# The guard of the q and k norms moves from a GpSimd clamp into VectorE's normalising instruction, as a minimum with 1e12

## The chip, the cores and the metric

The kernel runs on one core of a Trainium2 chip. The metric is the device time of one execution in microseconds (us), as a median of runs. The engines are TensorE (PE; PEld is its loading of weights), VectorE (DVE), ScalarE (ACT), GpSimd (POOL) and SyncE (SP, which only starts DMAs here). Each engine runs its own instructions in program order and waits for others at semaphores.

## The reference, cut to what matters

A residual block over 2048 tokens of width 128: softmax attention, a stack of local attention and feed-forward layers, linear attention, and the same stack again. One stack has six layers, and each layer first does this:

```
qkv = shift_tokens(x) @ Wqkv                    # 16 heads of 64
q = q / max(norm(q), 1e-12) * q_scale           # norm over the 64 elements of a head
k = k / max(norm(k), 1e-12) * k_scale
q, k = rotary(q, k)
attn = softmax(8 * q @ k^T over a window of 32 keys before and up to the token)
x = (attn @ v) @ Wo + x
```

A feed-forward layer follows. The change concerns the two lines with `max(norm, 1e-12)`, in both stacks (named f and g in the profile): twelve layers in all.

## The kernel before

`local_stack` does one stack. Its attention part goes over 16 tiles of 128 tokens, and over four steps (c = 0 to 3) in each tile: a step handles 8 heads of q or k (512 columns), in the order q, k, q, k. So a layer has 64 steps, numbered n = 4t + c, and the twelve layers have 768. The work is a software pipeline written out by hand: in step n every engine does a piece for step n, and later pieces for steps before it, always in the same order. All tiles on the way have two buffers (`b = c % 2`).

The chain of one step, by tile names:

- PE multiplies x by a slice of `wqkv` into `ps_qk` (L1171).
- ACT squares it into `sq` (L991), DVE sums the squares of each head into `ss`, 128x8 (L1083).
- POOL clamps: `sg = max(ss, 1e-24)` (L928), and takes `rn = sg ^ -0.5` (L931). An increment of `pl_sg` and a wait for it stand between the two.
- DVE normalises: `qh = ps_qk * rn`, with `rn` repeated over the 64 elements of a head (L1070). Then it makes the two rotary products `t1` and `t2` (L1097, L1099).
- POOL adds them into `qr` (L936). PE transposes `qr` (L1240), and ACT copies that into `qT` or `kT` (L1016, L1018, L1020).
- PE writes the mask and the scores (L1187, L1194), DVE takes the maximum `nmx` (L1076), ACT the exponentials `ex` (L1005), DVE the reciprocal `rd` and the product `pn` (L1087, L1090), PE transposes `pn` (L1176), ACT copies it to `pT` (L987), PE multiplies by v (L1232), ACT copies the result to `aT` (L1027).

In one step the orders of the engines are:

- DVE: `qh` of n-1, `nmx` of n-4, `ss` of n, `rd` and `pn` of n-5, `t1` and `t2` of n-1. Once a tile (c = 0) `xr` stands ahead of `qh` (L1066).
- POOL: `sg` of n, `rn` of n, `qr` of n-1.
- PE: `wqkv` product of n, transposes of `pn` of n-6, mask and scores of n-4, then in c = 0 and 2 a product for v (L1207), in c = 1 a transpose of x (L1160), in c = 3 the product with `wo` (L1214, 16 instructions), then the product with v of n-7 (L1232) and the transposes of `qr` of n-2 (L1240).
- ACT: copy of `pT`, squares, in c = 0 and 2 the copy of v, exponentials, copy of `qT` or `kT`, copy of `aT`.

The first 11 steps of a layer have no `wo` product, and the first few none of the later pieces. The mask and the scores in c = 0 and c = 2 wait for a copy to `kT`.

Of the kernel before, what the change touches and what calls it, by code (L numbers as in the profile page):

```python
# [9 lines left out]
ALU = mybir.AluOpType  # L10
# [3 lines left out]
P = 128  # L14
# [5 lines left out]
DH = 64  # L20
# [604 lines left out]
def local_stack(nc, tag, w, consts, xf, xa):  # L625
# [6 lines left out]
    with ExitStack() as ctx:  # L632
        sems, per_layer, ahead = [], {}, {}

        def sb(name, shape, dt=F32):
            return ctx.enter_context(nc.sbuf_tensor(f"{tag}_{name}", shape, dt))

        def sem(name, each=0, start=0):

            s = ctx.enter_context(nc.semaphore(f"{tag}_{name}"))  # L640
            sems.append(s)
            per_layer[s.num], ahead[s.num] = each, start
            return s

        def upto(s, L, n, by=1):

            return L * per_layer[s.num] + (n * by + (by + ahead[s.num]))

        def bank(i, n=1):
# [5 lines left out]
        ps_qk = banks[0:2]  # L655
# [29 lines left out]
        xT = sb("xT", [P, 2, P])  # L685
        sq = sb("sq", [P, 2, 512])
        ss = sb("ss", [P, 2, 8])
        sg = sb("sg", [P, 2, 8])
        rn = sb("rn", [P, 2, 8])
        qh = sb("qh", [P, 2, 512])  # L690
        t1 = sb("t1", [P, 2, 512])
# [39 lines left out]
        pe_v, act_v = sem("pe_v", 2 * NT, 3), sem("act_v", 2 * NT, 1)  # L731

        pe_qkv, act_sq, dv_ssq = sem("pe_qkv", STEPS), sem("act_sq", STEPS), sem("dv_ssq", STEPS, 2)
        pl_sg, pl_rn, dv_qh, dv_t2, pl_qr = (sem("pl_sg", STEPS), sem("pl_rn", STEPS, 2), sem("dv_qh", STEPS, 2),
                                             sem("dv_t2", STEPS), sem("pl_qr", STEPS, 2))
        pe_qkT, act_kprev, act_qk = sem("pe_qkT", STEPS, 2), sem("act_kprev", STEPS // 2), sem("act_qk", STEPS, 1)

# [165 lines left out]
        @block.gpsimd  # L903
        def _(pool):
            for s in (pl_rn, pl_qr):
                pool.sem_inc(s, ahead[s.num])
            pool.memset(minus_half[:], -0.5).then_inc(zeroed, 1)
            pool.memset(kT[:], 0.0).then_inc(zeroed, 1)

            def fold_rope(n, kind):  # L910

                pool.wait_ge(ld_scales, upto(ld_scales, n, 0, 32))
                whole = qk_scales[:, kind, :].unsqueeze(1).broadcast_to([P, NT, DH])
                halves = qk_scales[:, kind, :].rearrange("p (a b) -> p a b", a=2)[:, ::-1, :]
                pool.tensor_tensor(rope[:, 2 * kind, :, :], rope0[:, 2 * kind, :, :], whole, ALU.mult).then_inc(pl_rope, 1)
                for a in range(2):
                    sl = slice(a * 32, a * 32 + 32)
                    pool.tensor_tensor(rope[:, 2 * kind + 1, :, sl], rope0[:, 2 * kind + 1, :, sl],
                                       halves[:, a, :].unsqueeze(1).broadcast_to([P, NT, 32]),
                                       ALU.mult).then_inc(pl_rope, 1)  # L920

            def tile(L, t, q):
                for c in range(4):
                    n, b = 4 * t + c, c % 2
                    if real(t, c, 0):

                        pool.wait_ge(dv_ssq, upto(dv_ssq, L, n)).then_inc(own["pool"], 1)
                        pool.tensor_scalar(sg[:, b, :], ss[:, b, :], 1e-24, None, ALU.max).then_inc(pl_sg, 1)  # L928
                        pool.wait_ge(pl_sg, upto(pl_sg, L, n))
                        pool.wait_ge(dv_qh, upto(dv_qh, L, n - 2))  # L930
                        pool.tensor_tensor(rn[:, b, :], sg[:, b, :], minus_half[:], ALU.pow).then_inc(pl_rn, 1)  # L931
                    if real(t, c, 1):

                        pool.wait_ge(dv_t2, upto(dv_t2, L, n - 1))
                        pool.wait_ge(pe_qkT, upto(pe_qkT, L, n - 3))
                        pool.tensor_tensor(qr[:, 1 - b, :], t1[:, 1 - b, :], t2[:, 1 - b, :], ALU.add).then_inc(pl_qr, 1)  # L936

            def inverse_std(L, m, q):
                pool.wait_ge(dv_mv, upto(dv_mv, L, m)).then_inc(own["pool"], 1)
                pool.tensor_scalar(var[:, q, :], mv[:, q, :, 1], 1e-5, None, ALU.add).then_inc(pl_var, 1)  # L940
                pool.wait_ge(pl_var, upto(pl_var, L, m))
                pool.tensor_tensor(rstd[:, q, :], var[:, q, :], minus_half[:, 0:FT], ALU.pow).then_inc(pl_rstd, 1)

            def group(L, m, q):
                known = isinstance(m, int)
                if known and m == 0:
                    inverse_std(L, 0, 0)
                if not known or m + 1 < NF:
                    inverse_std(L, m + 1, 1 - q)
                if not known or 0 <= m - 2 < NF:  # L950

                    pool.wait_ge(ld_wf, upto(ld_wf, L, 0, 13 * 16))
                    pool.wait_ge(ld_f[q], upto(ld_f[q], L, (m - 2) >> 1, 16))
                    pool.tensor_tensor(fx[:, q, :, :], fx[:, q, :, :], b2[:].unsqueeze(1).broadcast_to([P, FT, D]),
                                       ALU.add).then_inc(pl_b2, 1)
                if known and m < 2:
                    pool.wait_ge(dv_t2, upto(dv_t2, L, STEPS - 1))
                    fold_rope(L + 1, m)

            pool.wait_ge(zeroed, 5)  # L960
            pool.wait_ge(ld_rope, 16)
            fold_rope(0, 0)
            fold_rope(0, 1)
            with pool.Fori(0, DEPTH) as L:
                layer(pool, tile, group, L, NT + 1)
# [88 lines left out]
        def _(dve):  # L1054
# [5 lines left out]
            def tile(L, t, q):  # L1060
                for c in range(4):
                    n, b = 4 * t + c, c % 2
                    if c == 0 and real(t - 3, 0, 0):
                        dve.wait_ge(pe_Wo, upto(pe_Wo, L, t - 3))
                        dve.wait_ge(ld_r[1 - q], upto(ld_r[1 - q], L, (t - 3) >> 1, 16))
                        dve.tensor_tensor(xr[:, 1 - q, :], ps_y[:, 0:P], xr[:, 1 - q, :], ALU.add).then_inc(dv_y, 1)  # L1066
                    if real(t, c, 1):

                        dve.wait_ge(pl_rn, upto(pl_rn, L, n - 1))
                        dve.tensor_tensor(heads(qh[:, 1 - b, :]), heads(ps_qk[1 - b][:]),  # L1070
                                          rn[:, 1 - b, :].unsqueeze(2).broadcast_to([P, 8, DH]), ALU.mult).then_inc(dv_qh, 1)
                    if real(t, c, 4):

                        dve.wait_ge(pe_s, upto(pe_s, L, n - 4))
                        dve.wait_ge(act_exp, upto(act_exp, L, n - 6))
                        dve.tensor_reduce(nmx[:, b, :].rearrange("p (h j) -> p h j", h=2),  # L1076
                                          ps_s[:, :, 0:2 * KEYS].rearrange("p h (j c) -> p h j c", j=2), AX.X, ALU.max,
                                          negate=True).then_inc(dv_max, 1)
                    if real(t, c, 0):

                        dve.wait_ge(act_sq, upto(act_sq, L, n))
                        dve.wait_ge(pl_rn, upto(pl_rn, L, n - 2))
                        dve.tensor_reduce(ss[:, b, :], heads(sq[:, b, :]), AX.X, ALU.add).then_inc(dv_ssq, 1)  # L1083
                    if real(t, c, 5):

                        dve.wait_ge(act_exp, upto(act_exp, L, n - 5))
                        dve.reciprocal(rd[:, 1 - b, :], sm[:, 1 - b, :]).then_inc(dv_rd, 1)  # L1087
                        dve.wait_ge(dv_rd, upto(dv_rd, L, n - 5))
                        dve.wait_ge(pe_pT, upto(pe_pT, L, n - 7))
                        dve.tensor_tensor(pn[:, 1 - b, :, :], ex[:, 1 - b, :, :],  # L1090
                                          rd[:, 1 - b, :].unsqueeze(2).broadcast_to([P, 4, KEYS]), ALU.mult).then_inc(dv_pn, 1)
                    if real(t, c, 1):

                        tj, cj = t + (c - 1) // 4, (c - 1) % 4
                        dve.wait_ge(dv_qh, upto(dv_qh, L, n - 1))
                        dve.wait_ge(pl_qr, upto(pl_qr, L, n - 3))
                        dve.tensor_tensor(heads(t1[:, 1 - b, :]), heads(qh[:, 1 - b, :]),  # L1097
                                          rope[:, 2 * KIND[cj], row(tj), :].broadcast_to([P, 8, DH]), ALU.mult)
                        dve.tensor_tensor(split(t2[:, 1 - b, :]), split(qh[:, 1 - b, :])[:, :, ::-1, :],  # L1099
                                          rope[:, 2 * KIND[cj] + 1, row(tj), :].broadcast_to([P, 8, DH]).rearrange(  # L1100
                                              "p h (a b) -> p h a b", a=2), ALU.mult).then_inc(dv_t2, 1)
# [599 lines left out]
```

## Time and profile before

| what | value |
|---|---|
| median of 3 runs | 5555.81 us (5553.79 to 5558.2) |
| the profiled execution | 5558.9 us |
| its span, first to last instruction | 5557.1 us |
| PE busy | 4778.2 us, 86% |
| DVE busy | 3995.7 us, 72% |
| ACT busy | 3633.8 us, 65% |
| POOL busy | 3288.9 us, 59% |

The span is what the rows below are read from. "Busy" counts an engine's own instructions. The costliest single line of the page is L931 on POOL: 744.8 us in each stack. The two stacks run from about 985 to 3160 us and from about 3365 to 5540 us.

### The profile page before, as it was taken

The page shows a single profiled execution, that of the slowest core. Times are in us where ns is not written, and L with a number is a line of the kernel's source. Part 1 is how long each engine was busy: PE and PEld are TensorE (multiplying, and loading weights), DVE is VectorE, ACT ScalarE, POOL GpSimd, SP SyncE. Part 2 cuts the span into 40 slices and gives each one's busy share as a digit, 9 for nine tenths or more (in the row PEclk, how much of TensorE's full clock was granted, in tenths as well). Part 3 has the DMA queues.
Part 4 walks back from the last instruction along what each step waited for, and adds up shares of the span by engine and source line. Part 5 has one row for each costly group of instructions (what it writes and reads, how often), then busy time and mean ns, then how long its engine had stood idle before and what let it go on. Part 6 is the DMA issues. An engine that isn't in the chain of part 4 may idle for free. (4 is left out here: it accounts for less than half of the span.)

```text
span 5557.1 us, 149601 instructions
## 1 busy us (share of the span) xinstructions
PE 4778.2 (86%) x45702; PEld 2962.8 (53%) x45796; DVE 3995.7 (72%) x8097; ACT 3633.8 (65%) x11776; POOL 3288.9 (59%) x2876
## 2 busy tenths in 40 slices
PE   5999998797998988979889666989989889798896
PEld 1333332465665665656656454655656656566565
DVE  7888885676776767767767546767767777677675
ACT  1777776675775757757667405757757667577674
POOL 3000000785876858858678406858858678587684
PEclk6999999899999999999999878999999999999998
DMA  0000000222222222222222202222222222222223
GB/s 13 1 2 1 2 1 16 80 56 73 50 65 65 50 74 55 50 74 56 69 56 57 79 6 83 57 74 50 66 65 51 74 57 53 71 56 66 61 53 89
DMA packets 332331, 288.41 MB, mean 52 GB/s; under 512 B 149102, under 2 KB 290964, under 8 KB 329748
## 3 DMA queue, kind: packets, MB, share of 16 engines
q1 hardware_dynamic: 331028, 281.93, 19.7%
q8 instruction: 254, 4.16, 0.3%
q14 instruction: 281, 2.30, 0.1%
q10 hardware_dynamic: 768, 0.02, 0.0%
HBM read 100.42 MB, written 30.41 MB: 24 GB/s over the span
## 5 line engine op out<-in xcount | busy, mean ns | idle before, releaser
L931 POOL TENSOR_TENSOR g_rn<-g_sg,g_minus_half 128x8 f32<-128x8 f32 x384 | 744.8, 1940 | 32.0
L931 POOL TENSOR_TENSOR f_rn<-f_sg,f_minus_half 128x8 f32<-128x8 f32 x384 | 744.8, 1939 | 32.0
L425 DVE TENSOR_REDUCE a_maxima<-a_max 128x1 f32<-128x512 f32 x1024 | 651.5, 686 | 148.4 <-PE a_max L539 111.3
L1005 ACT ACTIVATE g_ex<-g_bank,g_nmx 128x96 f32<-128x96 f32 x1536 | 502.6, 342 | 235.1 <-DVE g_nmx L1076 235.1
L1005 ACT ACTIVATE f_ex<-f_bank,f_nmx 128x96 f32<-128x96 f32 x1536 | 502.6, 342 | 234.6 <-DVE f_nmx L1076 234.5
L349 ACT ACTIVATE a_pex<-a_scores 128x512 f32<-128x512 f32 x1024 | 531.9, 607 | 160.2 <-PE a_scores L548 159.2
L1070 DVE TENSOR_TENSOR f_qh<-f_bank,f_rn 128x512 f32<-128x512 f32 x384 | 265.6, 692 | 370.5 <-POOL f_rn L931 370.5
L1070 DVE TENSOR_TENSOR g_qh<-g_bank,g_rn 128x512 f32<-128x512 f32 x384 | 265.6, 692 | 370.5 <-POOL g_rn L931 370.5
L936 POOL TENSOR_TENSOR f_qr<-f_t 128x512 f32<-128x512 f32 x384 | 485.6, 1265 | 11.5 <-DVE f_t L1099 11.5
L936 POOL TENSOR_TENSOR g_qr<-g_t 128x512 f32<-128x512 f32 x384 | 485.6, 1264 | 11.5 <-DVE g_t L1099 11.5
L1171 PE MATMUL g_bank<-g_wqkv,g_xT 128*128 128x512 f32 x768 | 410.5, 617 | 33.0 <-ACT g_xT L979 24.6
L1171 PE MATMUL f_bank<-f_wqkv,f_xT 128*128 128x512 f32 x768 | 410.2, 617 | 31.9 <-ACT f_xT L979 24.3
L928 POOL TENSOR_SCALAR f_sg<-f_ss 128x8 f32<-128x8 f32 x384 | 219.8, 572 | 339.0 <-DVE f_ss L1083 339.0
L928 POOL TENSOR_SCALAR g_sg<-g_ss 128x8 f32<-128x8 f32 x384 | 219.8, 572 | 337.4 <-DVE g_ss L1083 337.4
L280 POOL COPY a_v_head<-a_v_all 128x128 f32 (+1 forms) x16 | 4.6, 293 | 695.1 <-PE a_sums L557 695.1
L1240 PE MATMUL g_bank<-g_ident,g_qr 128*128 128x128 f32 x1536 | 254.1, 288 | 133.3 <-POOL g_qr L936 133.3
L1240 PE MATMUL f_bank<-f_ident,f_qr 128*128 128x128 f32 x1536 | 253.4, 288 | 132.9 <-POOL f_qr L936 132.9
L539 PE MATMUL a_max<-a_stackT 128*128 128x512 bf16 x963 | 347.6, 397 | 20.8 <-DVE a_maxima L425 12.6
L548 PE MATMUL a_scores<-a_stackT 128*128 128x512 bf16 x991 | 308.8, 382 | 27.7 <-ACT a_pex L349 20.6
L1005 ACT ACTIVATION_READ_ACCUMULATOR g_ex<-g_bank,g_nmx 128x1 f32 x1536 | 318.2, 207 | 0.0
L1005 ACT ACTIVATION_READ_ACCUMULATOR f_ex<-f_bank,f_nmx 128x1 f32 x1536 | 318.1, 207 | 0.0
L1083 DVE TENSOR_REDUCE f_ss<-f_sq 128x8 f32<-128x512 f32 x384 | 259.5, 676 | 49.0 <-ACT f_sq L991 35.0
(240 smaller groups left out, 12390.7 us busy)
## 6 DMA issues: line engine op xcount, KB each, us to landing
f_vw<-f_vt SPq DMA_DIRECT2D x96, 384.0 KB, 4.3
g_vw<-g_vt SPq DMA_DIRECT2D x96, 384.0 KB, 4.3
f_vw<-f_vt SPq DMA_DIRECT2D x96, 256.0 KB, 3.6
g_vw<-g_vt SPq DMA_DIRECT2D x96, 256.0 KB, 3.6
f_vw<-f_vt SPq DMA_DIRECT2D x96, 128.0 KB, 2.3
g_vw<-g_vt SPq DMA_DIRECT2D x96, 128.0 KB, 2.3
f_wqkv<-in_f_Wqkv_dram SPq DMA_DIRECT2D x7, 1536.0 KB, 9.3
g_wqkv<-in_f_Wqkv_dram SPq DMA_DIRECT2D x7, 1536.0 KB, 9.5
```

The source lines that it names most:

```text
L349: act.activation(pex[:, kt % 2, i % NG, :], ps_s[i % 3][:], ACT.Exp).then_inc(act_ex, 1)
L425: dve.tensor_reduce(maxima[:, m // 4, m % 4:m % 4 + 1], ps_max[m % 3][:], AX.X, ALU.max).then_inc(dv_max, 1)
L539: pe.matmul(ps_max[m % 3][:], stackT[:, slot, 0, P * (m // 4):P * (m // 4) + P], stackT[:, slot, 1, GQ * (m % 4):GQ * (m % 4) + GQ], start ...
L548: pe.matmul(ps_s[i % 3][:], stackT[:, slot, 1, P * kt:P * kt + P], stackT[:, slot, 0, GQ * g:GQ * g + GQ], start=True, stop=True).then_inc ...
L928: pool.tensor_scalar(sg[:, b, :], ss[:, b, :], 1e-24, None, ALU.max).then_inc(pl_sg, 1)
L931: pool.tensor_tensor(rn[:, b, :], sg[:, b, :], minus_half[:], ALU.pow).then_inc(pl_rn, 1)
L936: pool.tensor_tensor(qr[:, 1 - b, :], t1[:, 1 - b, :], t2[:, 1 - b, :], ALU.add).then_inc(pl_qr, 1)
L1005: last = act.activation(ex[:, b, u, :], ps_s[:, h, KEYS * jj:KEYS * jj + KEYS], ACT.Exp, bias=nmx[:, b, u:u + 1], accum_out=sm[:, b, u:u + 1])
L1070: dve.tensor_tensor(heads(qh[:, 1 - b, :]), heads(ps_qk[1 - b][:]), rn[:, 1 - b, :].unsqueeze(2).broadcast_to([P, 8, DH]), ALU.mult).then_ ...
L1083: dve.tensor_reduce(ss[:, b, :], heads(sq[:, b, :]), AX.X, ALU.add).then_inc(dv_ssq, 1)
L1171: pe.matmul(ps_qk[b][:], xT[:, q, :], wqkv[:, at:at + 512], start=True, stop=True).then_inc(pe_qkv, 1)
L1240: last = pe.transpose(ps_qkT[:, P * j:P * j + P], qr[:, b, P * j:P * j + P], ident[:])
```

## The change

POOL's clamp, its tile `sg` and its semaphore are gone; POOL raises `ss` itself to -0.5. DVE's normalising instruction takes the minimum of `rn` and 1e12 before it multiplies. It was a TENSOR_TENSOR with the PSUM tile as its first input and `rn` as its second; it is now a SCALAR_TENSOR_TENSOR with `rn` as its first input, the constant 1e12, and the PSUM tile as its second.

```diff
-        sg = sb("sg", [P, 2, 8])
...
-        pl_sg, pl_rn, dv_qh, dv_t2, pl_qr = (sem("pl_sg", STEPS), sem("pl_rn", STEPS, 2), sem("dv_qh", STEPS, 2),
+        pl_rn, dv_qh, dv_t2, pl_qr = (sem("pl_rn", STEPS, 2), sem("dv_qh", STEPS, 2),
...
                         pool.wait_ge(dv_ssq, upto(dv_ssq, L, n)).then_inc(own["pool"], 1)
-                        pool.tensor_scalar(sg[:, b, :], ss[:, b, :], 1e-24, None, ALU.max).then_inc(pl_sg, 1)
-                        pool.wait_ge(pl_sg, upto(pl_sg, L, n))
                         pool.wait_ge(dv_qh, upto(dv_qh, L, n - 2))
-                        pool.tensor_tensor(rn[:, b, :], sg[:, b, :], minus_half[:], ALU.pow).then_inc(pl_rn, 1)
+                        pool.tensor_tensor(rn[:, b, :], ss[:, b, :], minus_half[:], ALU.pow).then_inc(pl_rn, 1)
...
-                        dve.tensor_tensor(heads(qh[:, 1 - b, :]), heads(ps_qk[1 - b][:]),
-                                          rn[:, 1 - b, :].unsqueeze(2).broadcast_to([P, 8, DH]), ALU.mult).then_inc(dv_qh, 1)
+                        dve.scalar_tensor_tensor(out=heads(qh[:, 1 - b, :]), in0=rn[:, 1 - b, :].unsqueeze(2).broadcast_to([P, 8, DH]),
+                                                 scalar=1e12, in1=heads(ps_qk[1 - b][:]), op0=ALU.min, op1=ALU.mult).then_inc(dv_qh, 1)
```

## Rows read from the trace of the kernel before

**Rows 1.** Chain of waits over the span: waiter, releaser, us in total, times, longest.

```profile
DVE f_qh L1070 <- POOL f_rn L931: 370.5, 384, 2.2
```

**Rows 2.** Timeline of DVE, steady steps: start, duration, engine, line, names, shapes, idle before.

```profile
1203.21 0.69 DVE L1070 TENSOR_TENSOR f_qh<-f_bank,f_rn 128x512 f32<-128x512 f32 x1 [0.95 <-POOL f_rn L931]
...
1204.29 0.68 DVE L1083 TENSOR_REDUCE f_ss<-f_sq 128x8 f32<-128x512 f32 x1
...
1205.08 0.56 DVE L1090 TENSOR_TENSOR f_pn<-f_ex,f_rd 128x384 f32<-128x384 f32 x1
1205.56 0.68 DVE L1097 TENSOR_TENSOR f_t<-f_qh,f_rope 128x512 f32<-128x512 f32 x1
...
1207.80 0.69 DVE L1070 TENSOR_TENSOR f_qh<-f_bank,f_rn 128x512 f32<-128x512 f32 x1 [0.95 <-POOL f_rn L931]
...
1216.97 0.69 DVE L1070 TENSOR_TENSOR f_qh<-f_bank,f_rn 128x512 f32<-128x512 f32 x1 [0.95 <-POOL f_rn L931]
```

**Rows 3.** Timeline of POOL in the same step.

```profile
1205.16 0.58 POOL L928 TENSOR_SCALAR f_sg<-f_ss 128x8 f32<-128x8 f32 x1 [0.75 <-DVE f_ss L1083]
1205.83 1.94 POOL L931 TENSOR_TENSOR f_rn<-f_sg,f_minus_half 128x8 f32<-128x8 f32 x1
1207.74 1.27 POOL L936 TENSOR_TENSOR f_qr<-f_t 128x512 f32<-128x512 f32 x1
```

**Rows 4.** Timeline of POOL and DVE, first two steps of a layer.

```profile
996.46 0.25 POOL L928 TENSOR_SCALAR f_sg<-f_ss 128x8 f32<-128x8 f32 x1 [1.18 <-DVE f_ss L1083]
996.79 1.67 POOL L931 TENSOR_TENSOR f_rn<-f_sg,f_minus_half 128x8 f32<-128x8 f32 x1
...
999.97 0.50 POOL L928 TENSOR_SCALAR f_sg<-f_ss 128x8 f32<-128x8 f32 x1 [1.52 <-DVE f_ss L1083]
...
1000.29 0.68 DVE L1099 TENSOR_TENSOR f_t<-f_qh,f_rope 128x512 f32<-128x512 f32 x1
...
1000.56 1.94 POOL L931 TENSOR_TENSOR f_rn<-f_sg,f_minus_half 128x8 f32<-128x8 f32 x1
```

**Rows 5.** Timeline of PE over one tile of steady steps.

```profile
1204.50 0.66 PE L1240 MATMUL f_bank<-f_ident,f_qr 128*128 128x128 f32 x4
...
1209.02 0.69 PE L1232 MATMUL f_bank<-f_pT,f_vw 128*64 128x64 f32 x16
1209.64 0.66 PE L1240 MATMUL f_bank<-f_ident,f_qr 128*128 128x128 f32 x4
...
1213.85 0.66 PE L1240 MATMUL f_bank<-f_ident,f_qr 128*128 128x128 f32 x4
...
1216.64 0.69 PE L1232 MATMUL f_bank<-f_pT,f_vw 128*64 128x64 f32 x16
1218.31 0.65 PE L1240 MATMUL f_bank<-f_ident,f_qr 128*128 128x128 f32 x4 [0.98 <-POOL f_qr L936]
...
1220.42 0.34 PE L1187 MATMUL f_bank<-f_mask_bf,f_ident_bf 128*128 128x192 bf16 x2 [0.16 <-ACT f_kT L1020]
...
1222.85 0.66 PE L1240 MATMUL f_bank<-f_ident,f_qr 128*128 128x128 f32 x4
```

**Rows 6.** Windows of the steady part: us, busy by engine, PE clock, DMA.

```profile
1150.00:1278.00 128.00, 119.79 (x1376) 80.09 (x1376) 101.84 (x202) 99.68 (x369) 105.36 (x84) 1.00 0.22 54
```

**Rows 7.** Timeline of ACT in the step after the `wo` product.

```profile
1212.22 0.60 ACT L991 ACTIVATE f_sq<-f_bank 128x512 f32<-128x512 f32 x1
```

**Rows 8.** Groups of DVE by line and shape: count, busy us, mean ns, idle before.

```profile
L1140 DVE SCALAR_TENSOR_TENSOR g_ag<-g_bank,g_b,g_gl 128x256 f32<-128x256 f32 x96 | 45.9, 483 | 80.6 <-ACT g_gl L1041 80.6
...
L1130 DVE TENSOR_TENSOR g_fy<-g_bank,g_fx 128x256 f32<-128x256 f32 x48 | 20.2, 422 | 16.4 <-DMA xf<-g_fy 11.5 <-PE g_bank L1271 3.1 <-POOL g_fx L954 1.8
...
L1483 DVE TENSOR_SCALAR b_kp<-b_bank 128x512 f32<-128x512 f32 x16 | 11.1, 692 | 13.0 <-PE b_bank L1590 13.0
```

**Rows 9.** Timeline of DVE and of POOL in a feed-forward part.

```profile
1309.96 1.26 DVE L1140 SCALAR_TENSOR_TENSOR f_ag<-f_bank,f_b,f_gl 128x256 f32<-128x256 f32 x3 [3.17 <-ACT f_gl L1041]
...
1310.40 2.48 POOL L918 TENSOR_TENSOR f_rope<-f_rope,f_qk_scales 128x512 f32<-128x512 f32 x2
```

## The prediction

> **What bounds the kernel now.** I read the waits first, then the timelines of DVE and POOL over a few steps, then PE's. The waits say where the changed lines stand: DVE waits for `rn` before every `qh`, 370.5 us in 384 steps of a stack [rows 1], 741 us in both. Whether that idle time is the bound, the timeline must say. It does: one `qh` starts at 1203.21, the next at 1207.80, a period of 4.59 us [rows 2], and the same period holds in practically every steady step, whatever PE has to do in it. Follow what ends last: `ss` starts 1.08 after `qh`; POOL's `sg` starts 0.87 after `ss`, at 1205.16, and ends at 1205.74; the power runs from 1205.83 to 1207.77; `qh` follows at 1207.80 [rows 2, 3]. So the step is a closed loop of DVE and POOL, with the clamp in it: 1.08 + 0.87 + 0.58 + 0.09 + 1.94 + 0.03 = 4.59. DVE idles 0.95 in it; its own work is 3.64 a step.
>
> PE is nearly as full: 119.79 of 128 us, at a granted clock of 1.00, that is 2.4 GHz [rows 6]. Its starts give what it needs when nothing holds it. A tile is four steps: 5.14 us with the `wo` product (1204.50 to 1209.64), 4.21 with a v product (to 1213.85), 3.40 with the transpose of x (to 1216.64 + 0.62, the 0.62 as from 1209.02 to 1209.64), and 4.21 again (the trace shows 4.54, 1218.31 to 1222.85, with a wait of 0.33 for `kT` inside) [rows 5]. Sum 16.96 against 18.36 for four periods. PE has only 1.40 us of idle time in a tile, and the loop can't gain more there.
>
> **What goes, and what it costs: POOL.** How long the power takes depends on DVE. In a layer's first step DVE is idle and the clamp takes 0.25, the power 1.67. In the second step the clamp takes 0.50 and the power 1.94; that power starts at 1000.56, under a product with two SBUF inputs that ends at 1000.97, and ends 1.53 after that [rows 4]. In the steady step the clamp starts 0.08 after `pn` and ends 0.10 after `pn` ends (1205.64); the power starts under `t1`, which ends at 1206.24, and again ends 1.53 later, though `t2` follows `t1` without a gap [rows 2, 3]. So a POOL instruction that meets a DVE instruction with two SBUF inputs is held until that one ends, and slips in before the next one.
>
> Without the clamp the power takes its place, at 1205.16, and is held by `pn` in place of `t1`. It ends at 1205.64 + 1.53 = 1207.17, and `qh` starts at 1207.20: 0.60 earlier, period 3.99, and 2.91 from `ss` to `qh`. The bounds for the gain of the loop: if it took 1.94 from its start, 0.67; if 1.67, 0.94; if it had to wait for `t1` after all, nothing (a rival below). I take 0.60, since three pairs of rows fit it. The semaphore and the wait that go too lie inside the 0.09. `qr` comes as early after `qh` as before, since POOL starts it when the power ends; POOL's load falls from 3.8 to 3.3 a step. No DMA or wait is added.
>
> The Trainium skill, "SBUF — State Buffer", section "Who interferes with whom", says that a DVE instruction with two SBUF inputs contends with a GpSimd instruction that reads SBUF, and that one with at most one SBUF input doesn't. The trace agrees with the first half by 0.25 against 0.50. By the page's other half the new `qh`, with one input in PSUM, stays clear of `qr`.
>
> **What is added: DVE.** `qh` takes 0.692 as a TENSOR_TENSOR; the trace has no 512-wide SCALAR_TENSOR_TENSOR. A 256-wide one with a pointer scalar takes 483 ns against 422 for a TENSOR_TENSOR of that size, 61 more; a two-operation TENSOR_SCALAR with constants, from PSUM, takes 692 at 512 [rows 8]. So the new one costs 0.69 if the 61 ns belong to the pointer and 0.75 if they don't. I take 0.69, the row with constants; 0.75 makes the loop 4.05. Below 0.69 I see no reason, as the elements are as many.
>
> **What is late next.** If only the loop counted, a layer would gain 0.33 in its first step (clamp plus gap) and 0.60 in 63 more, 38.1 us, or 458 us in twelve layers: 5101. PE doesn't allow it. Its tile of 16.96 is longer than 4 x 3.99 = 15.96. And it can't be quite dense, for one chain goes round through all engines once a tile. From the mask of c = 2 PE needs 2.43 to the end of its step (1220.42 to 1222.85) and 5.14 for the step with `wo`. From there the squares of c = 0 end 3.18 later (1209.64 to 1212.82) [rows 5, 7]; 0.03 on, `ss` starts, then 2.91 to `qh`. And 3.45 after `qh`, by way of `nmx`, exponentials and `kT`, comes the next mask of c = 2 (1216.97 to 1220.42) [rows 2, 5]. Sum: 2.43 + 5.14 + 3.21 + 2.91 + 3.45 = 17.14. Before, it was 17.74 and hidden under 18.36. A steady tile gains 18.36 - 17.14 = 1.22, not 2.40.
>
> **Sum.** A layer has 64 steps. First step 0.33. Steps 2 to 11 have no `wo` product; a tile of PE without it is about 15 us, under 15.96, so each gains the loop's 0.60: 6.0. The other 53 steps are 13.25 tiles, at 1.22: 16.2. At the end of the attention part PE is about 0.8 further behind DVE than before (the chain above puts it there; an estimate), and that is paid in the drain. 0.33 + 6.0 + 16.2 - 0.8 = 21.7 a layer, 260 us in twelve. Feed-forward parts, both other attentions and DMAs only shift. The profiled execution took 5558.9 with a span of 5557.1, 3.1 above the median shown: 5558.9 - 260 = 5299, or 5296 by the median. I predict 5296.
>
> Bounds: with PE dense (16.96) and nothing paid in the drain, 0.33 + 6.0 + 18.6 = 24.9 a layer, 5257. With `qh` at 0.75, the early steps gain 0.54 and the chain is 17.20: 20.3 a layer, 5312. The likeliest case alone: 5250 to 5345.
>
> **Rivals.**
>
> *No slack between PE and the loop.* Then each step costs the longer of the two: 5.14 + 4.21 + 3.99 + 4.21 = 17.55. Gain 0.33 + 6.0 + 13.25 x 0.81 - 0.8 = 16.3 a layer: 5361. For it speaks that the engines share two buffers only; against it, that the loop today holds 4.59 through a PE step of 5.14.
>
> *The new instruction runs at half rate.* 256 elements more cost 270 ns in rows 8 (692 - 422), so 512 at half rate add 0.54. The loop becomes 4.53, a gain of 0.06 a step, about 46 us: 5510. The skill's "Vector Engine (DVE) Microarchitecture Reference", section "Points that are easy to get wrong", says that this form halves its throughput with two SBUF sources that aren't bf16. Here one source is in PSUM, so by its letter the rule doesn't apply, and no row shows the case.
>
> *The change doesn't do what it says.* If the power must wait for `t1` although it starts under `pn`, it ends where it ends now, and nothing moves: 5556. Against it: the clamp, and the power in rows 2 and 3, slip in between two such products.
>
> *Slower: the new `qh` collides with `qr`.* POOL starts `qr` 0.06 before `qh`, for 1.27. If the new form, with `rn` as its first input, is held until `qr` ends, each step grows by 1.21: 3.99 + 1.21 = 5.20, 0.61 longer than now, 468 us in 768 steps: 6024. It decides from 0.60 us more in `qh`. Against it: three instructions of this form, one input in PSUM and one in SBUF, take 1.26 in all while POOL works on `rope` [rows 9]. Only the places of the inputs are swapped.
>
> **Chances.** Forecast 0.70; no slack 0.13; half rate 0.07; nothing moves 0.04; collision 0.04; the rest, 0.02, for something slower unseen. The range runs from 5245, just under PE dense, to 5400, beyond the case without slack, and leaves out the last four: 0.17. Within 0.2% (11 us) is what can't be told from no change. Faster 0.90, same 0.04, slower 0.06.
>
> **What the profile after must show.** POOL's power about 2.0 long, ending 1.53 after `pn`; `qh` at 0.69; 2.91 from `ss` to `qh` when nothing else holds it. The period no longer constant: four steps of about 17.1, a gap of a few tenths before the mask of c = 2, `ss` waiting for `sq` or `nmx` for the scores after the `wo` step. DVE's wait for `rn` down from 0.95 to about 0.35 a step, and PE's busy share up. Wrong it would be if `qh` were longer, if `ss` waited in most steps, or if the clock fell below 1.00 in the denser stretch.

## The result, and the profile after

The kernel after takes 5336.36 us as a median of 4 runs (5324.37 to 5340.76), the kernel before 5557.01 (5553.79 to 5559.11). The ratio is 0.960, with a 95% interval of 0.9583 to 0.9617. 5296 was forecast, 40 us lower; the gain is 221 us where 260 was forecast.

The page of the kernel after, its parts 1 and 5 (busy us, share of the span, instructions; then line, engine, names, count, busy us, mean ns, idle before):

```profile
span 5333.0 us, 148063 instructions
...
PE 4757.5 (89%) x45702; PEld 2949.2 (55%) x45796; DVE 4038.5 (76%) x8097; ACT 3633.9 (68%) x11776; POOL 2862.2 (54%) x2108
...
L928 POOL TENSOR_TENSOR f_rn<-f_ss,f_minus_half 128x8 f32<-128x8 f32 x384 | 750.8, 1955 | 459.7 <-DVE f_ss L1080 371.0
...
L1067 DVE SCALAR_TENSOR_TENSOR f_qh<-f_rn,f_bank 128x512 f32<-128x512 f32 x384 | 264.0, 687 | 133.3 <-POOL f_rn L928 122.6
...
L1073 DVE TENSOR_REDUCE f_nmx<-f_bank 128x4 f32<-128x384 f32 x384 | 213.0, 555 | 127.5 <-PE f_bank L1191 126.1
```

POOL lost 768 instructions, the clamps, and 427 us of busy time. The others do the same work in a shorter span. The new instruction takes 687 ns, the old one 692. DVE's wait for `rn` fell from 370.5 us a stack [rows 1] to 122.6, and DVE now waits 126.1 us for the scores, as the prediction said it would after the `wo` step. A window inside the steady part of both kernels, before and after (columns as in rows 6; the window of rows 6 itself reaches beyond the steady part of the kernel after, whose last `qh` of that layer starts at 1264.2):

```profile
1100.00:1228.00 128.00, 120.03 (x1378) 80.07 (x1376) 101.84 (x203) 99.82 (x370) 105.02 (x84) 1.00 0.22 54
...
1100.00:1228.00 128.00, 126.66 (x1459) 84.92 (x1457) 110.07 (x217) 105.86 (x393) 94.65 (x61) 1.00 0.24 58
```

PE works 126.66 of 128 us where it was 120.03; the granted clock is 1.00 in both, the level of 2.4 GHz.

The loop of DVE and POOL, in steps where PE holds nothing up (timeline of the kernel after; start, duration):

```profile
1202.33 0.56 DVE L1087 TENSOR_TENSOR f_pn<-f_ex,f_rd 128x384 f32<-128x384 f32 x1
...
1202.50 1.90 POOL L928 TENSOR_TENSOR f_rn<-f_ss,f_minus_half 128x8 f32<-128x8 f32 x1 [1.08 <-PE f_bank L1237]
...
1204.43 0.69 DVE L1067 SCALAR_TENSOR_TENSOR f_qh<-f_rn,f_bank 128x512 f32<-128x512 f32 x1 [0.33 <-POOL f_rn L928]
...
1205.50 0.68 DVE L1080 TENSOR_REDUCE f_ss<-f_sq 128x8 f32<-128x512 f32 x1
...
1206.29 0.56 DVE L1087 TENSOR_TENSOR f_pn<-f_ex,f_rd 128x384 f32<-128x384 f32 x1
1206.36 2.00 POOL L928 TENSOR_TENSOR f_rn<-f_ss,f_minus_half 128x8 f32<-128x8 f32 x1 [0.72 <-DVE f_ss L1080]
...
1208.39 0.69 DVE L1067 SCALAR_TENSOR_TENSOR f_qh<-f_rn,f_bank 128x512 f32<-128x512 f32 x1 [0.33 <-POOL f_rn L928]
```

From `ss` to `qh` it is 1208.39 - 1205.50 = 2.89 (2.91 foreseen), and the period 1208.39 - 1204.43 = 3.96 (3.99). The power starts 0.17 after `pn` in one step and 0.07 after it in the next, and takes 1.90 and 2.00: its end is 1.51 after the end of `pn` both times. So it is held by `pn`, as worked out. (The releaser "PE f_bank L1237" in the second row is an inference by time; by the code that instruction waits for DVE alone. Where the profile names an engine that the code doesn't, the code decides.)

I read the starts of `qh` of the first layer of the first stack, before and after, into this table ("tile" is the 60th start less the 12th, over 12):

| | before | after | foreseen after |
|---|---|---|---|
| first `ss` to first `qh` | 2.91 | 2.59 | 2.58 |
| next 11 steps | 48.7 | 41.95 | about 42.4 (ten at 0.60 less, one at 1.22 / 4) |
| a steady tile of four steps | 18.35 | 17.35 | 17.14 |
| periods in a tile | four of 4.59 | 3.96, 3.96, 5.20, 4.21 | not all alike |
| last `qh` to the next layer's first `ss` | 70.9 | 72.1 | 0.8 more |

The layer went from 361.1 to 342.1 us. One row of the table is off: the tile, by 0.2 us.

### The profile page after: what moved, and what is told of

It is laid out like the page before. It is cut to its first block and busy times, and to the rows that moved or that the text cites. A ratio compares the mean times of both kernels' runs of the same rounds, so it can differ in the third digit from the quotient of the medians.

```text
span 5333.0 us, 148063 instructions
## 1 busy us (share of the span) xinstructions
PE 4757.5 (89%) x45702; PEld 2949.2 (55%) x45796; DVE 4038.5 (76%) x8097; ACT 3633.9 (68%) x11776; POOL 2862.2 (54%) x2108
## 5 line engine op out<-in xcount | busy, mean ns | idle before, releaser
L928 POOL TENSOR_TENSOR g_rn<-g_ss,g_minus_half 128x8 f32<-128x8 f32 x384 | 750.9, 1956 | 464.0 <-DVE g_ss L1080 379.5
L928 POOL TENSOR_TENSOR f_rn<-f_ss,f_minus_half 128x8 f32<-128x8 f32 x384 | 750.8, 1955 | 459.7 <-DVE f_ss L1080 371.0
L1002 ACT ACTIVATE f_ex<-f_bank,f_nmx 128x96 f32<-128x96 f32 x1536 | 505.6, 349 | 42.4 <-DVE f_nmx L1073 41.3
L933 POOL TENSOR_TENSOR g_qr<-g_t 128x512 f32<-128x512 f32 x384 | 486.1, 1266 | 17.7 <-DVE g_t L1096 17.7
L933 POOL TENSOR_TENSOR f_qr<-f_t 128x512 f32<-128x512 f32 x384 | 486.1, 1266 | 17.7 <-DVE f_t L1096 17.7
L1067 DVE SCALAR_TENSOR_TENSOR g_qh<-g_rn,g_bank 128x512 f32<-128x512 f32 x384 | 264.0, 688 | 133.3 <-POOL g_rn L928 122.6
L1067 DVE SCALAR_TENSOR_TENSOR f_qh<-f_rn,f_bank 128x512 f32<-128x512 f32 x384 | 264.0, 687 | 133.3 <-POOL f_rn L928 122.6
L1073 DVE TENSOR_REDUCE g_nmx<-g_bank 128x4 f32<-128x384 f32 x384 | 213.0, 555 | 132.8 <-PE g_bank L1191 131.3
L1073 DVE TENSOR_REDUCE f_nmx<-f_bank 128x4 f32<-128x384 f32 x384 | 213.0, 555 | 127.5 <-PE f_bank L1191 126.1
L1080 DVE TENSOR_REDUCE g_ss<-g_sq 128x8 f32<-128x512 f32 x384 | 260.5, 678 | 51.5 <-ACT g_sq L988 34.3
L1229 PEld LDWEIGHTS g_bank<-g_pT,g_vw 128*64 128x64 f32 x6144 | 210.3, 137 | 157.5 <-issue 129.6
```

Of the source, the lines that this page charges most:

```text
L928: pool.tensor_tensor(rn[:, b, :], ss[:, b, :], minus_half[:], ALU.pow).then_inc(pl_rn, 1)
L1002: last = act.activation(ex[:, b, u, :], ps_s[:, h, KEYS * jj:KEYS * jj + KEYS], ACT.Exp, bias=nmx[:, b, u:u + 1], accum_out=sm[:, b, u:u + 1])
L1067: dve.scalar_tensor_tensor(out=heads(qh[:, 1 - b, :]), in0=rn[:, 1 - b, :].unsqueeze(2).broadcast_to([P, 8, DH]), scalar=1e12, in1=heads(p ...
L1229: last = pe.matmul(ps_o[r, at:at + BLK], vw[:, p, blk, P * j + DH * h:P * j + DH * h + DH], pT[:, 1 - b, 2 * h + jj, BLK * blk:BLK * blk + ...
```

## The experiments

Each ratio below is to runs of the kernel before that were taken with it. "Tile" is measured as above, in the first layer of each kernel's own profile; it is the same within 0.02 in all twelve layers.

**Which chain holds the tile.** The timeline after, over one tile. These rows make up one chain (L976, in c = 1, is ACT's copy of the transposed x into `xT`):

```profile
1194.03 0.66 PE L1237 MATMUL f_bank<-f_ident,f_qr 128*128 128x128 f32 x4
...
1196.56 1.12 PE L1204 MATMUL f_bank<-f_wqkv,f_xT 128*128 128x512 f32 x2
...
1197.89 0.59 ACT L996 COPY f_vt<-f_bank 128x512 f32<-128x512 f32 x1 [0.69 <-PE f_bank L1204]
...
1200.28 0.56 PE L1191 MATMUL f_bank<-f_kT,f_qT 64*64 64x96 f32 x16
...
1200.91 0.56 DVE L1073 TENSOR_REDUCE f_nmx<-f_bank 128x4 f32<-128x384 f32 x1
...
1201.35 0.29 ACT L976 COPY f_xT<-f_bank 128x128 f32<-128x128 f32 x1
1201.51 0.38 ACT L1002 ACTIVATE f_ex<-f_bank,f_nmx 128x96 f32<-128x96 f32 x1
...
1202.79 0.33 ACT L1015 COPY f_kT<-f_kT 128x128 f32<-128x128 f32 x1
...
1203.15 0.59 ACT L1017 COPY f_kT<-f_bank 128x512 f32<-128x512 f32 x1
...
1203.79 0.34 PE L1184 MATMUL f_bank<-f_mask_bf,f_ident_bf 128*128 128x192 bf16 x2 [0.19 <-ACT f_kT L1017]
...
1206.22 0.66 PE L1237 MATMUL f_bank<-f_ident,f_qr 128*128 128x128 f32 x4
...
1211.36 0.66 PE L1237 MATMUL f_bank<-f_ident,f_qr 128*128 128x128 f32 x4
```

The prediction had the next mask of c = 2 at 3.45 after a `qh`, since `nmx` follows `qh` at 0.61. Here `qh` starts at 1200.21, but `nmx` only at 1200.91, when the scores of c = 1 end (1200.28 + 0.56). The mask stands 1203.79 - 1194.03 = 9.76 after the end of the `wo` step, not 9.57 (3.21 + 2.91 + 3.45). With 2.43 and 5.14 the chain is 17.33. It doesn't pass through the power at all. Over all twelve layers the `nmx` that follows such a `qh` starts 0.7 after it and 0.07 after the end of the scores; in the kernel before, every `nmx` of the steady steps started 0.61 after its `qh`, and 0.7 us or more after the scores. This is theory A; theory B is the prediction's chain, with something small added.

*POOL adds where it raised to a power (norms left out; q and k are scaled wrongly).*

```diff
-pool.tensor_tensor(rn[:, b, :], ss[:, b, :], minus_half[:], ALU.pow).then_inc(pl_rn, 1)
+pool.tensor_tensor(rn[:, b, :], ss[:, b, :], minus_half[:], ALU.add).then_inc(pl_rn, 1)
```

> GpSimd adds in place of raising to a power, so q and k are scaled wrongly (the norm is left out); GpSimd's instruction falls from about 2.0 us to some 0.6. Theory A, a steady tile is set by a chain that goes from PE's scores of c = 1 over the maximum, the exponentials and the copies to kT to the mask of c = 2 and does not pass through the power: the steady tile stays at 17.3 us, only the first steps of a layer gain, about 4 us a layer: 5336 - 45 = 5290. Theory B, the chain of the prediction, through the squares, the power and qh: the tile falls to PE's 16.96, 0.38 x 13 x 12 = 59 us more: 5231.

Measured: 5307.21 us, ratio 0.9551 (0.9535 to 0.9567). The tile is 17.33. The instruction takes 0.56 where it took 2.00. So a POOL instruction that is far shorter moves the steady tile by nothing, and theory B falls. In the first layer the first `qh` comes 1.42 earlier after the first `ss` and the 11 steps behind it gain 2.05, together 3.5 where about 4 were expected. Over twelve layers the two profiles give 39 us there; 7.5 of them are lost again between the layers, and 29 show in the medians.

*The small copy inside `kT` goes to where ACT waits for v.* It reads and writes only columns whose scores are done by then.

```diff
                         act.activation(sq[:, b, :], ps_qk[b][:], ACT.Square).then_inc(act_sq, 1)
+                    if c % 2 == 0 and real(t, c, 1):
+                        tj, cj = t + (c - 1) // 4, (c - 1) % 4
+                        pairs = slice(4 * HALF[cj], 4 * HALF[cj] + 4)
+                        act.wait_ge(pe_s, upto(pe_s, L, 4 * tj - 3 + 2 * HALF[cj]))
+                        act.copy(kT[:, pairs, 0:WINDOW], kT[:, pairs, P:P + WINDOW]).then_inc(act_kprev, 1)
...
-                            act.copy(kT[:, pairs, 0:WINDOW], kT[:, pairs, P:P + WINDOW]).then_inc(act_kprev, 1)
```

> ACT's small copy inside kT moves from between the exponentials and the kT copy to right after the squares of the step before, where ACT waits for the v product. Theory A: the chain of 17.33 us loses 0.33 and PE's own 16.96 is left: 0.35 x 13 x 12 = 55 us, 5281, and PE's wait before the mask of c = 2 goes from 0.44 to about 0.1. Rival: that wait is filled by another one right behind it (aT, pT or the scores), and the tile stays at 17.3: 5336. Theory B says 17.14 at least as the bound of the power's chain, less 0.33 for the same copy: 5281 too, so this run tells only whether the wait for kT is the bound.

Measured: 5270.54 us, ratio 0.9481 (0.9466 to 0.9497), tile 17.00. This is the fastest version of the study with the whole computation in it, 66 us under the kernel after. By the two profiles 53 of the 66 lie in the steady tiles, where 55 were expected; 8 more lie between the stacks, where the edit changes nothing (see the granted clock there, below). The timeline at the same place:

```profile
1184.79 0.37 ACT L1008 ACTIVATE f_ex<-f_bank,f_nmx 128x96 f32<-128x96 f32 x1
...
1185.11 0.61 ACT L1022 COPY f_kT<-f_bank 128x512 f32<-128x512 f32 x1
...
1185.32 0.60 PE L1178 MATMUL f_bank<-f_ident,f_pn 128*96 128x128 f32 x4
...
1185.78 0.34 PE L1189 MATMUL f_bank<-f_mask_bf,f_ident_bf 128*128 128x192 bf16 x2
```

The copy to `kT` follows the last exponential directly, and the mask follows the transposes of `pn` after 0.46, with no wait named.

*The same edit in the kernel before.*

> The early copy inside kT in the kernel before, with its clamp. The loop of DVE and POOL holds 4.59 a step, the chain through kT is 17.3 a tile and hidden under 18.36: period 4.59, no change, 5557 within 11. If the kT wait had a price of its own in the kernel before, the 66 us that the same edit gave after the change would show here in part.

Measured: 5552.61 us, ratio 0.9993 (0.9984 to 1.0003), period 4.59 throughout. What shortened the tile by 0.35 after the change gives nothing without it: the period is still that of DVE and POOL, and the chain of 17.33 is hidden under 18.36.

**PE's part and ACT's part of it.** Two kernels leave out 15 of the 16 instructions of the product with v (so the attention output is mostly stale in those steps), once in c = 1 and once in c = 0:

```diff
-                        for jj in range(2):
+                        short = c == 1        # c == 0 in the other kernel
+                        for jj in range(1 if short else 2):
...
-                            for blk in range(2):
-                                for h in range(2):
+                            for blk in range(1 if short else 2):
+                                for h in range(1 if short else 2):
```

> PE leaves out 15 of the 16 instructions of the product with v in the steps c = 1, about 0.58 us of its work a tile. In theory A that work stands outside the chain (it comes after the scores of c = 1 and ends before the mask of c = 2 is allowed): tile 17.3, time 5336. Rival C, the tile is PE's work plus a fixed wait, wherever the work stands: 0.58 x 13 x 12 = 90 us less, 5246.

> The same 15 instructions left out in the steps c = 0, where they stand on theory A's chain: that chain falls to 16.75, and the next one, through squares and power (17.12 by the rows of after), takes over: 0.22 x 13 x 12 = 34 us less, 5302. If the power's chain were no bound at all, 0.58 a tile: 5246. Rival C says 5246 here as for c = 1.

Measured: 5329.78 us for c = 1 (ratio 0.9593, 0.9577 to 0.9609; tile 17.35) and 5327.49 for c = 0 (0.9583, 0.9567 to 0.9599; tile 17.32). Neither differs from the kernel after by more than its own runs differ (5324.37 to 5340.76). That the tile is PE's work plus a fixed wait is refuted. But theory A had said 5302 for c = 0, and missed. The timeline of that kernel shows why:

```profile
1181.11 0.58 ACT L996 COPY f_vt<-f_bank 128x512 f32<-128x512 f32 x1 [0.71 <-PE f_bank L1204]
...
1182.43 0.60 PE L1173 MATMUL f_bank<-f_ident,f_pn 128*96 128x128 f32 x4
...
1182.55 0.35 ACT L1002 ACTIVATE f_ex<-f_bank,f_nmx 128x96 f32<-128x96 f32 x1
...
1183.14 0.33 PE L1184 MATMUL f_bank<-f_mask_bf,f_ident_bf 128*128 128x192 bf16 x2
...
1184.56 0.29 ACT L976 COPY f_xT<-f_bank 128x128 f32<-128x128 f32 x1
1184.70 0.39 ACT L1002 ACTIVATE f_ex<-f_bank,f_nmx 128x96 f32<-128x96 f32 x1
```

From the copy of v in c = 0 to the first exponential of c = 1 ACT works without a gap, 3.59 us here and 1201.51 - 1197.89 = 3.62 in the kernel after. PE gained 0.58 and lost most of it at once, since the mask of c = 1 waits for the exponentials of c = 0 (1183.14 is 0.71 after the transposes, not 0.44; counted from the copy of v the mask comes only 0.11 earlier). So two chains are tied there: ACT's own work, and PE's with `nmx`. That is theory A2, and two more kernels test it. In one ACT copies 8 of 128 columns of `pT` in c = 1 (most attention weights stale there); in the other PE's product is short in c = 0 as well.

```diff
-act.copy(pT[0:KEYS, b, :, :], ps_pT[0:KEYS, :].rearrange("p (u q) -> p u q", u=4)).then_inc(act_pT, 1)
+w = 8 if c == 1 else P
+act.copy(pT[0:KEYS, b, :, 0:w], ps_pT[0:KEYS, :].rearrange("p (u q) -> p u q", u=4)[:, :, 0:w]).then_inc(act_pT, 1)
```

> ACT copies 8 of 128 columns of each head's pT in the steps c = 1, so a quarter of the attention weights is left stale; some 0.3 us of ACT's work goes. Theory A2, after the run that shortened PE's product in c = 0 to no effect: from the v product of c = 0 to the mask of c = 2 two chains are tied within 0.05, ACT's own unbroken work (v copy, exponentials, qT, aT, pT, squares, xT, exponentials) and PE's with nmx of c = 1. Shortening ACT's alone moves the tile by 0.05 at most: 17.30 to 17.35, 5336. If ACT's work alone were the bound: 17.05, 0.3 x 13 x 12 = 47 us less, 5289.

> Both at once: 15 of 16 instructions of the product with v left out in c = 0 and pT short in c = 1. Theory A2: both of the tied chains are shorter now; the mask of c = 1 can move only 0.11 earlier, until it waits for the exponentials of c = 0, so the tile falls by about 0.1, to 17.2 (16 us, 5320), more than the sum of the two alone. If something third holds the tile: 17.31 as in the single ones.

Measured: 5329.43 us for ACT alone (0.9592, 0.9576 to 0.9608; tile 17.32), and 5315.88 for both (0.9564, 0.9548 to 0.958; tile 17.20). Each alone moves the tile by 0.03; both together by 0.15, where 0.1 was expected. A2 stands. What holds the tile at 17.20 is in the timeline of that kernel, from a `qh` of c = 1 to the `ss` of c = 0 in the next tile:

```profile
1185.47 0.69 DVE L1068 SCALAR_TENSOR_TENSOR f_qh<-f_rn,f_bank 128x512 f32<-128x512 f32 x1 [0.33 <-POOL f_rn L928]
...
1186.09 0.56 DVE L1074 TENSOR_REDUCE f_nmx<-f_bank 128x4 f32<-128x384 f32 x1
...
1188.93 0.34 PE L1185 MATMUL f_bank<-f_mask_bf,f_ident_bf 128*128 128x192 bf16 x2 [0.16 <-ACT f_kT L1018]
...
1191.37 0.66 PE L1239 MATMUL f_bank<-f_ident,f_qr 128*128 128x128 f32 x4
...
1196.50 0.66 PE L1239 MATMUL f_bank<-f_ident,f_qr 128*128 128x128 f32 x4
...
1199.08 0.60 ACT L989 ACTIVATE f_sq<-f_bank 128x512 f32<-128x512 f32 x1
...
1199.79 0.68 DVE L1081 TENSOR_REDUCE f_ss<-f_sq 128x8 f32<-128x512 f32 x1
```

The mask is back at 3.46 after `qh`, and `nmx` at 0.62. So here the prediction's own chain closes: 2.44 (1188.93 to 1191.37) + 5.13 (to 1196.50) + 3.29 (to 1199.79) + 2.88 (to the next `qh`, 1185.47 + 17.20) + 3.46 = 17.20. Its 3.29 was foreseen as 3.21: `ss` starts 0.11 after the squares end and not 0.03, because DVE is busy with `nmx`, which waited for the scores. PE's chain through the scores arrives at the same time (`nmx` starts 0.07 after them), and no run separates the two.

*The early copy and the short product in c = 1 together.*

> The early copy on top of the change, and the product with v cut to one instruction in c = 1, where it gave nothing without the early copy. If the early copy has made PE's own work the bound (16.96 to 17.0 a tile), the cut counts now: the tile falls until the chain through the power, 17.12 - 0.33 = 16.8, holds it: 0.2 x 13 x 12 = 31 us, 5240. If ACT's work or the kT wait is still the bound at 17.0: 5270.

Measured: 5273.28 us, ratio 0.9488 (0.9473 to 0.9504), tile 16.99, no better than the early copy alone. The mask of c = 2 stands 0.52 after the transposes of `pn` here, where it was 0.46:

```profile
1186.21 0.64 PE L1178 MATMUL f_bank<-f_ident,f_pn 128*96 128x128 f32 x4
...
1186.73 0.34 PE L1189 MATMUL f_bank<-f_mask_bf,f_ident_bf 128*128 128x192 bf16 x2
```

PE saved 0.58 before the transposes of `pn`, but they start 2.90 after the mask of c = 1 (2.97 with the early copy alone), since `qr` and `pn` come no earlier; and the mask stands 0.66 after the copy to `kT` begins (1186.07), as in the kernel after (0.64). So in the fastest version two bounds nearly meet: the chain of A2 less 0.33, at 17.00, and PE's own work, 16.96. What I had expected of the early copy, that it would leave only PE's own work as the bound, was wrong.

**What the parts of the change cost.** Without any guard and with the old DVE instruction, and with both guards (the clamp kept, the new instruction used):

```diff
 # no guard: the kernel after, with the instruction of the kernel before
-dve.scalar_tensor_tensor(..., scalar=1e12, in1=heads(ps_qk[1 - b][:]), op0=ALU.min, op1=ALU.mult)
+dve.tensor_tensor(heads(qh[:, 1 - b, :]), heads(ps_qk[1 - b][:]), rn..., ALU.mult)
 # both guards: the kernel before, with the same two lines the other way round
```

> The change without its minimum: no guard at all, and VectorE keeps the old TENSOR_TENSOR. If the new form costs nothing: as after, 5336, within 11 us. If the form itself gives or takes some hundredths of a us in the loop, that shows in the first 11 steps of a layer alone: at 0.03 a step about 4 us, not to be told.

> The kernel before with VectorE's new instruction, the clamp on GpSimd kept. If all of the gain is GpSimd's: a period of 4.59 and 5557. The first steps gained 0.63 where the sum said 0.60; if the 0.03 are the new instruction's, the period is 4.56 and the time 5557 - 0.03 x 768 = 5534.

Measured: no guard 5325.37 us (5324.13 to 5342.93), ratio 0.9585 (0.9571 to 0.9598), tile 17.35; the interval overlaps that of the kernel after, 0.9583 to 0.9617, and the tile is the same. Both guards 5559.81, ratio 1.0009 (1.0 to 1.0018), periods as in the kernel before, 4.04 in the first three steps of a layer and 4.59 later. So the new instruction costs nothing and gives nothing, and all of the gain is the clamp's. The two medians without and with the minimum differ by 11 us, but the steps don't: 41.95 for the first 11 and 17.35 for a tile in both. The 0.03 by which the loop came out shorter than foreseen isn't the new instruction's. Most of it is the power's: undisturbed it takes 1.65 in both kernels without the clamp, and 1.67 with it. Why is open.

## Why the prediction was right, and what was mis-sized

- *The loop of DVE and POOL is the bound at 4.59, the clamp is in it.* Right: with both guards the period stays 4.59, and without the clamp the early steps fall to 3.96.
- *The power, moved under `pn`, ends 1.53 after it; gain 0.60 a step.* Right: 1.51 (1.50 or 1.51 in all 708 steps in which it starts under `pn`), and 0.63.
- *The new instruction at 0.69.* Right, 686 to 691 ns in the 384 of the first stack; the 61 ns of rows 8 belong to the pointer scalar or to something else that isn't here. Half rate and a collision with `qr` didn't come: `qr` starts 0.06 before `qh` as before, and takes 1266 ns.
- *Loop alone would give 458 us, PE and the chain through `kT` allow less.* Right in kind. This is why a step 0.63 shorter in the loop gives 0.25 a step in a tile.
- *"Sum: 2.43 + 5.14 + 3.21 + 2.91 + 3.45 = 17.14."* This is the term that was mis-sized: the tile is 17.35, so a tile gains 1.0 and not 1.22. The sum took the mask of c = 2 at 3.45 after `qh`, an offset read where DVE's loop was late enough to set `nmx`. Once the loop is faster, the scores of c = 1 set `nmx`, and ACT's unbroken work behind the v copy arrives at the same time: 3.58 in place of 3.45. A smaller part is `ss` waiting for `nmx` after the `wo` step, 3.29 in place of 3.21. 13.25 tiles x 0.21 x 12 = 33 us of the 40 missed.
- *0.8 us a layer paid in the drain.* Right as a mean: from the last `qh` of a layer to the first `ss` of the next it is 0.88 more over the ten such places, though from 0.6 less to 2.9 more in single ones (1.15 in the first).
- *No slack between PE and the loop* (17.55, 5361). The measured 5336 is nearer to this rival than to the forecast, but its mechanism isn't what the rows show: PE goes through the step with the transpose of x in 3.41 (1198.24 to 1201.65), while the loop needs 3.96. The tile of 17.35 lies between the two for another reason.

The two profiled executions, added up by their parts, give the whole of the miss. Gains in us, foreseen by the prediction's terms over twelve layers, and measured:

| | foreseen | measured |
|---|---|---|
| first `ss` to first `qh` | 4.0 | 3.7 |
| next 11 steps | 75.7 | 79.3 |
| other 52 steps | 190.3 | 157.7 |
| between layers, ten places | -8.0 | -8.8 |
| ahead of, between and behind the stacks | -1.6 | -7.8 |
| sum | 260 | 224.1 |

The line before the sum holds what the prediction had left out with "only shift", less the two drains at the ends of the stacks. Between the stacks the kernel after took some 8 us longer than the kernel before, with the same code there. The windows of before and after, from the last `qh` of the first stack to the first `ss` of the second:

```profile
3090.40:3373.90 283.50, 164.60 (x889) 125.71 (x886) 126.82 (x346) 47.70 (x111) 51.89 (x63) 0.72 0.20 58
...
2971.50:3263.20 291.70, 174.05 (x911) 129.76 (x910) 127.06 (x347) 49.20 (x115) 51.82 (x63) 0.70 0.19 57
```

PE's granted clock was at its lower level, 1.2 GHz, for 156.5 us of the first and 173.3 of the second. This goes with the execution and not with the change: the kernel with the short product in c = 1 took 281.4 us there (152.6 at the lower level), the one without a guard 292.8 (176.7), and the others lie between, from 283.2 with 156.5 to 291.7 with 176.5. The clock fell in the first steps of some layers too: in the four layers of the kernel after that have 6.8 us at the lower level among the next 11 steps, these took 43.3 to 43.6, and 42.0 to 42.2 in the other eight. No run changes the clock alone, so that it is the cause stays likely and not shown. But the 11.4 us between 281.4 and 292.8 are as much as the medians of those kernels differ that keep the power and have a tile of 17.3, 5325 to 5336.

## What to carry to other kernels

When a closed loop is shortened, list every other closed chain of the same repeat and add each up from starts, also those that don't pass through the changed engine: the longest of them, not the mean load of the busiest engine, is the new period. An offset between two instructions may be used in such a sum only if the row shows that it is a dependence; one read where the second was waiting for something else will be too short or too long. After the change look again at edits that gave nothing before it: the same moved copy was worth nothing before and 0.35 us a tile, some 53 us in all, after.

## What the runs showed of the hardware

A small GpSimd instruction that reads SBUF and starts under a VectorE instruction with two SBUF inputs ends at a fixed time after that instruction, however long it has already waited. In the kernel after, the power starts 0.06 to 0.17 after `pn` and takes 1.89 to 2.01, but in all 708 such steps it ends 1.50 or 1.51 after `pn`; undisturbed it takes 1.65. The addition put in its place ends 0.06 after `pn` in all of them, and takes 0.20 undisturbed; the clamp ended 0.10 after `pn` and took 0.25. So in each case some 0.15 of the instruction has passed when the hold ends. It isn't held by the next VectorE instruction of that kind, though that one starts 0.08 before `pn` ends. A GpSimd duration in such a place is thus partly a wait: the clamp's 0.58 was 0.25 of work, and removing it gave 0.63 a step because the power moved to an earlier instruction of VectorE.

Two VectorE forms cost the same here: the TENSOR_TENSOR with an input from PSUM took 692 ns at 128x512, and the SCALAR_TENSOR_TENSOR that does a minimum with a constant besides took 687. The minimum was free.
